# Two counting pairs in front of the gathered bodies, the preparing stage's waits moved into the next program, and the last stage of a graph kernel in one pass by quads

## The reference, cut to what matters

```python
# layer 0: message passing with a GRU cell
msg = (x[src] @ W_msg.T + b_msg) + edge_embed[clip(edge_type, 0, 8)]
messages = segment_sum(msg, dst, N)
x = layernorm(x + gru_cell(messages, x))
# layer 1: edges weighted by a gated score
proj = x @ fc_weight.T
el, er = proj[src], proj[dst]
e = sum(leaky_relu(el + er, 0.2) * a, -1)
w = sigmoid(e * sigmoid(sum(el * er, -1)))
neigh = segment_sum(x[src] * w, dst, N) / max(deg, 1)
x = layernorm(x + (1 + eps) * x + neigh)
```

## Time and profile before

| what | us |
|---|---|
| median of three runs | 3278.78 |
| lowest and highest | 3277.06 and 3279.28 |
| the profiled execution, its own time | 3269.84 |
| its span in the profile | 3268.0 |
| busy in the span: PE, DVE, ACT, POOL | 2154.1, 2508.1, 1592.7, 2135.2 |
| mean granted TensorE clock, as a share of full speed | 0.772 |

### The profile page before, as it was taken

One profiled execution on the slowest core, in us unless ns is written; L12 is line 12 of the kernel. 1 busy time (PEld: TensorE's weight loads), 2 busy tenths in 40 slices (PEclk: granted clock), 3 DMA queues, 4 the chain that ended last, 5 costly groups with the idle time before them and its releaser, 6 DMA issues. The chain is left out here.

```text
span 3268.0 us, 64802 instructions
## 1 busy us (share of the span) xinstructions
PE 2154.1 (66%) x13842; PEld 1733.9 (53%) x13842; DVE 2508.1 (77%) x12778; ACT 1592.7 (49%) x3458; POOL 2135.2 (65%) x2191
## 2 busy tenths in 40 slices
PE   1399999999989745555555555555655555555653
PEld 1277777777754445454444454454555545545552
DVE  6577777777735678888888888888888888888877
ACT  2265555555543345445445454445454544544541
POOL 2456766667720067777777777777777777777772
PEclk9999999999999766667667667767566666676665
DMA  7222222222220465655555565665565565566562
GB/s 142 79 57 65 73 65 70 71 67 70 68 71 1 146 182 158 168 163 158 168 163 158 165 166 158 162 166 161 159 170 161 158 167 164 157 169 164 155 169 65
DMA packets 357854, 424.88 MB, mean 130 GB/s; under 512 B 174156, under 2 KB 242134, under 8 KB 357733
## 3 DMA queue, kind: packets, MB, share of 16 engines
q0 software_dynamic: 103728, 266.13, 29.7%
q1 hardware_dynamic: 251793, 156.64, 18.3%
q10 hardware_dynamic: 2212, 0.60, 0.1%
HBM read 399.44 MB, written 23.70 MB: 129 GB/s over the span
## 5 line engine op out<-in xcount | busy, mean ns | idle before, releaser
L1407 POOL DMA_INDIRECT got<-rows,idx x1624 | 1546.5, 952 | 538.7 <-issue 509.8
L1573 PE MATMUL sum_ps<-whot,got 128*128 128x128 f32 x3264 | 690.1, 381 | 642.3 <-DVE whot L1419 573.2
L1573 PEld LDWEIGHTS sum_ps<-whot,got 128*128 128x128 f32 x3264 | 594.0, 273 | 730.5 <-DVE whot L1419 641.0
L735 POOL DMA_INDIRECT got<-x_rows,idx x532 | 540.5, 1016 | 255.9 <-issue 161.2
L1566 PE MATMUL er_ps<-win,hot_t 128*128 128x128 bf16 x4932 | 528.6, 285 | 260.7 <-ACT hot_t L1517 238.4
L886 ACT CAST work<-c_ps 128x318 bf16<-128x318 f32 x1092 | 454.9, 431 | 398.7 <-PE c_ps L962 391.1
L1475 DVE CUSTOM_DVE_ANT_0 pr_s<-got,er_ps 128x128 f32<-128x128 f32 x1624 | 370.0, 283 | 363.8 <-DMA got<-rows,idx 357.9
L1566 PEld LDWEIGHTS er_ps<-win,hot_t 128*128 128x128 bf16 x4932 | 468.9, 133 | 303.6 <-ACT hot_t L1517 268.2
L913 PE MATMUL span_ps<-x_parts,work 128*126 128x393 bf16 x2756 | 611.4, 332 | 0.0
L1419 DVE TENSOR_SCALAR whot<-iota_f,dl,w_s 128x128 f32<-128x128 f32 x1632 | 459.0, 358 | 0.3 <-ACT w_s L1522 0.3
L1547 ACT ACTIVATE r_s<-er_ps 128x512 f32<-128x512 f32 x406 | 242.3, 597 | 373.2 <-DVE er_ps L1487 371.2
(11 more groups left out here) (239 smaller groups left out, 1879.3 us busy)
## 6 DMA issues: line engine op xcount, KB each, us to landing
work<-dst_row SPq DMA_DIRECT2D x413, 256.0 KB, 4.0
got<-rows,idx POOLq DMA_INDIRECT x1624
win<-parts SPq DMA_DIRECT2D x118, 96.0 KB
got<-x_rows,idx POOLq DMA_INDIRECT x532
idx<-src_rows SPq DMA_DIRECT2D x413, 2.0 KB, 4.0
parts<-split SPq DMA_DIRECT2D x13, 384.0 KB, 2.9
x_rows<-x_parts SPq DMA_DIRECT2D x1, 4641.0 KB
rows<-nodes SPq DMA_DIRECT2D x13, 256.0 KB, 3.1
```

The lines of the kernel that those rows point to most:

```text
L735: pool.indirect_dma_start(got[:, c, i, 0:3 * D], None, x_rows, bass.IndirectOffsetOnAxis(ap=idx[:, c, i:i + 1], axis=0)).then_inc(gathered ...
L1407: pool.indirect_dma_start(got[:, c, i, :], None, rows, bass.IndirectOffsetOnAxis(ap=idx1[:, c, i:i + 1], axis=0)).then_inc(gathered[c], 16)
L1573: mm = pe.matmul(sum_ps[:, 0:P], got[:, c, i, D:2 * D], whot[:, c, i, :], start=(c == 0 and i == 0), stop=(c == NS - 1 and i == STEP - 1))
```

## The change

Five things are done.

1. SP stores `x_rows` in two halves, the first as soon as VectorE's first half is ready, and the three waits at the end of its program stand at the start of its next one. Three tables (`dst_t`, `type_h`, `src_i`) share the room of others, and `first_k` and its like live on into the next stage, since they are still being stored.
2. POOL clears `counts` first, waits for the earlier stores (which read `sums`' and `nodes`' room), and then clears `sums`.
3. LEAD = 2 pairs stand in front of the rounds and none behind them; the wait for the cleared tables is made by VectorE in the first pair that adds.
4. ScalarE multiplies `nodes` by `c_x` in front of its loop of the edge stage, 13 steps of a quad each.
5. The last stage is one pass: four PSUM buffers; product and sum in one step for each tile; the root of each quad by ScalarE, with the bound as its bias; reciprocal and offset by VectorE one quad later; and the normalising by ScalarE (scale and bias from the tables) two quads later, for the last quad by VectorE. POOL does nothing there.

The diff, cut to its core:

```diff
@@ preparing, SP @@
-                    sp.wait_ge(lo_cut, 2)
-                    sp.dma_start(x_rows[0:xf * LO, :].rearrange("(b p) f -> p b f", p=LO),
-                                 x_parts[0:LO, 0:xf, 0:3 * D]).then_inc(x_out, 16)
+                    for i, (b0, b1) in enumerate(half_b):
+                        bm = min(b1, xf)
+                        sp.wait_ge(lo_cut, i + 1)
+                        sp.dma_start(x_rows[b0 * LO:bm * LO, :].rearrange("(b p) f -> p b f", p=LO),
+                                     x_parts[0:LO, b0:bm, 0:3 * D]).then_inc(x_out, 16)
...
-                    sp.wait_ge(left_out, 16 * (2 + (br > 0)))
-                    sp.wait_ge(dst_out, 48)
-                    sp.wait_ge(tables_out, 48)
@@ counting, SP and POOL @@
+                    sp.wait_ge(left_out, 16 * (2 + (CT % ROWS > 0)))
+                    sp.wait_ge(dst_out, 48)
+                    sp.wait_ge(tables_out, 48)
...
                     pool.memset(nodes[:, ft:NTL, :], 0.0).then_inc(nodes_set, 1)
+                    pool.memset(counts[:, 0:NPAD], 0.0).then_inc(zeroed0, 1)
+                    pool.wait_ge(left_out, 16 * (2 + (CT % ROWS > 0)))
+                    pool.wait_ge(dst_out, 48)
                     pool.memset(sums[:, 0:NPAD], 0.0).then_inc(zeroed0, 1)
-                    pool.memset(counts[:, 0:NPAD], 0.0).then_inc(zeroed0, 1)
@@ counting, VectorE (ScalarE and PE alike) @@
                     make_pair(0, True)
-                    dve.wait_ge(zeroed0, 3)
+                    for k in range(1, LEAD):
+                        make_pair(k, False)
                     with dve.Fori(0, ROUNDS) as r:
                         for p in range(ROUND):
-                            make_pair(ROUND * r + p + 1, False, p, r)
-                    with dve.Fori(ROUNDS * ROUND + 1, PAIRS) as k:
-                        make_pair(k, False)
+                            make_pair(ROUND * r + p + LEAD, False, p, r)
@@ edges, ScalarE @@
+                    for q in range(NQ):
+                        t = slice(q * QUAD, (q + 1) * QUAD)
+                        act.activation(nodes[:, t, :], nodes[:, t, :], ACT.Copy, scale=c_x[:]).then_inc(scaled, 1)
                     with every_body(act) as k:
@@ last stage, ScalarE, VectorE and SP as they are now @@
+                    def root(q):
+                        act.wait_ge(agreed, QUAD * (q + 1))
+                        act.activation(rstd[:, q * QUAD:(q + 1) * QUAD], moments[:, q * QUAD:(q + 1) * QUAD, 1],
+                                       ACT.Sqrt, bias=low_bound[:]).then_inc(rooted, 1)
...
+                    def normalise(q):
+                        act.wait_ge(shifted, q + 1)
+                        for t in range(q * QUAD, (q + 1) * QUAD):
+                            act.activation(nodes[:, t, :], nodes[:, t, :], ACT.Identity, scale=rstd[:, t:t + 1],
+                                           bias=offset_s[:, t:t + 1]).then_inc(finished_act, 1)
...
+                    for q in range(NQ):
+                        root(q)
+                        if q >= 2:
+                            normalise(q - 2)
+                    normalise(LAST - 1)
...
+                    def scale_of(q):
...
+                        dve.wait_ge(rooted, q + 1)
+                        dve.reciprocal(rstd[:, t], rstd[:, t]).then_inc(inverse, 1)
+                        dve.wait_ge(inverse, q + 1)
+                        dve.scalar_tensor_tensor(out=offset_s[:, t], in0=moments[:, t, 0], scalar=-1.0,
+                                                 in1=rstd[:, t], op0=ALU.mult, op1=ALU.mult).then_inc(shifted, 1)
...
+                        for i in range(QUAD):
+                            t = q * QUAD + i
+                            dve.scalar_tensor_tensor(out=nodes[:, t, :], in0=m_ps[:, q % 4, i, :],
+                                                     scalar=rdeg[:, t:t + 1], in1=nodes[:, t, :],
+                                                     op0=ALU.mult, op1=ALU.add).then_inc(mixed, 1)
...
+                        if q >= 1:
+                            scale_of(q - 1)
...
+                    scale_of(LAST)
+                    dve.wait_ge(shifted, NQ)
+                    for t in range(LAST * QUAD, NTL):
+                        dve.tensor_scalar(nodes[:, t, :], nodes[:, t, :], rstd[:, t:t + 1], offset_s[:, t:t + 1],
+                                          ALU.mult, ALU.add).then_inc(finished, 1)
...
+                    for at in range(0, ft, 4):
+                        m = min(4, ft - at)
+                        wait_for(at + m)
+                        sp.dma_start(out[at * NODES:(at + m) * NODES, :].rearrange("(t p) f -> p t f", p=NODES),
+                                     nodes[:, at:at + m, :]).then_inc(stored, 16)
```

More of the change, by code:

```diff
@@ L48 @@
 PER_ROUND = 3
+LEAD = 2
 LN_EPS = 1e-5
@@ L897, in _ @@
                     copy_pair(0, True)
+                    for k in range(1, LEAD):
+                        copy_pair(k, False)
                     with act.Fori(0, ROUNDS) as r:
                         for p in range(ROUND):
-                            copy_pair(ROUND * r + p + 1, False, p, r)
-                    with act.Fori(ROUNDS * ROUND + 1, PAIRS) as k:
-                        copy_pair(k, False)
+                            copy_pair(ROUND * r + p + LEAD, False, p, r)
                     copy_sums(CGN - 2, 0)
@@ L980, in _ @@
                     count_pair(0, True)
+                    for k in range(1, LEAD):
+                        count_pair(k, False)
                     pe.wait_ge(zeroed0, 3)
@@ L1599, in graph_layers @@
         with ExitStack() as ph:
-            mean_s = sb("mean_s", [NODES, QUAD, D], F32, ph)
-            m_ps = psum("m_ps", [NODES, 2, QUAD, D], F32, ph)
+            m_ps = psum("m_ps", [NODES, 4, QUAD, D], F32, ph)
+            low_bound = sb("low_bound", [NODES, 1], F32, ph)
+            offset_s = sb("offset_s", [NODES, NTL], F32, ph)
+            bound_set = sem("bound_set")
             m_turned = sem("m_turned")
-            steps = sem("steps")
-            spread = sem("spread1")
+            mixed = sem("mixed")
+            stated = sem("stated")
+            agreed = sem("agreed")
+            rooted = sem("rooted")
+            inverse = sem("inverse")
+            shifted = sem("shifted")
             finished = sem("finished")
+            finished_act = sem("finished_act")
             stored = sem("stored")
-            finished_pool = sem("finished_pool")
-            S = 2 + 2 * QUAD
-            HERE = NTL * 3 // 4 // QUAD * QUAD + QUAD if NQ > 4 else NTL
-            def normalise(eng, tiles, done):
-                for t in tiles:
-                    eng.tensor_scalar(nodes[:, t, :], nodes[:, t, :], moments[:, t, 0:1], rstd[:, t:t + 1],
-                                      ALU.subtract, ALU.mult).then_inc(done, 1)
+            LAST = NQ - 1
             with nc.Block() as block:
@@ L1652, in _ @@
-                    dve.wait_ge(steps, S * NQ + 1)
-                    dve.tensor_scalar(rstd[:], moments[:, :, 1], LN_EPS, None, ALU.add).then_inc(spread, 1)
-                    dve.wait_ge(spread, 2)
-                    dve.reciprocal(rstd[:], rstd[:]).then_inc(spread, 1)
-                    dve.wait_ge(spread, 3)
-                    dve.sem_inc(spread, 1)
-                    normalise(dve, range(0, HERE), finished)
-                @block.gpsimd
-                def _(pool):
-                    pool.wait_ge(spread, 4)
-                    normalise(pool, range(HERE, NTL), finished_pool)
+                            dve.wait_ge(mixed, q * QUAD + i + 1)
@@ L1667, in _, with wait_for @@
                     n = 0
-                    starts = sorted(range(0, ft, 4), key=lambda t: t - (HERE if t >= HERE else 0))
-                    for at in starts:
+                    def wait_for(tiles):
+                        sp.wait_ge(finished_act, min(tiles, LAST * QUAD))
+                        if tiles > LAST * QUAD:
+                            sp.wait_ge(finished, tiles - LAST * QUAD)
+                    for at in range(0, ft, 4):
                         m = min(4, ft - at)
-                        if at >= HERE:
-                            sp.wait_ge(finished_pool, at - HERE + m)
-                        else:
-                            sp.wait_ge(finished, at + m)
+                        wait_for(at + m)
                         sp.dma_start(out[at * NODES:(at + m) * NODES, :].rearrange("(t p) f -> p t f", p=NODES),
```

67 lines of the change are left out of this document (30 added, 37 removed).

## The result

The changed kernel takes 3261.86 us, median of 7 executions, beside 3277.06 for the kernel before, timed together with it: ratio 0.9946 (0.9934 to 0.9957), 17.7 us less (14.1 to 21.6). The ratio is an estimate from all executions; the two medians alone differ by 15.2 us. Timed again later, the pair came to 0.9966 (0.9952 to 0.9979), 11.1 us less (6.9 to 15.7), 3259.01 beside 3270.95. The second time the kernel before ran 6.1 us faster than the first, the changed one 2.9.

A forecast was written before the change was run, and what follows sets the result against it. PE bounds the rounds, POOL's gathers the edge stage, VectorE the last stage, SP's store queue the seam. Terms 0 + 3.2 - 13.0 = -9.8 us from 3278.78 give 3269.0; range 3265 to 3273, eight in ten 3261 to 3277.

The forecast's parts named there:

- Seam, -6.9: After preparing: splitting the x_parts store ends it 3.7 us earlier, moving three waits saves 3.2; together 6.9 us.
- the transfer is the same bytes from the same partitions, so it ends 3.7 us earlier: Seam's store: the first half is ready 3.7 us sooner, so the whole transfer ends that much earlier.
- Rival E: Seam: halves slowed or a second large store costs SP, PE starts up to 3.7 us later; 3273; chance 0.10.
- Two pairs in front, 0: End of counting: the left-over body's gathers, no longer under the lone pair, give back the seam's 6.9 us: 0.
- rival D: Left-over body's bursts: the clock drops and stays low into the update stage; with 40 us, 3289; chance 0.05.
- B: Rival at counting's end: left-over gathers start earlier, seam's 6.9 us stay; -16.7, 3262; sign: products end by 945; chance 0.14.
- Edge stage, +3.2: Start of edge stage: 13 ScalarE scalings, 8.0 us, delay VectorE; POOL pauses once, near 1190: +3.2 (1.5 to 4.9).
- Last stage, -13.0: Last stage in one pass: quads of 2.64 us, then ScalarE's root and eight steps; -13.0 us (-15 to -11).
- 0.47 for four aggregations: Last stage: part of VectorE's old quad of 2.76 us, kept at 0.47 us in the new quad of 2.64.
- Rival C: Last stage: narrow steps cost full length, quad 3.1 us, 6 us more than forecast; -4, 3275; chance 0.15.

The follow-up runs named there:

- the run of the pairs alone: The kernel before with two pairs in front of the rounds and none behind, nothing else: ratio 1.0036 (1.0023 to 1.0050), 11.8 us slower.
- the first eight runs: Follow-up runs up to the combined kernel, in which every kernel, that before included, took about 4.28 ms; ratios between 0.9939 and 0.9995.
- one of the texts above: Text of the timing run of the kernel before with VectorE's loop of rounds 112 instructions further on: ratio 1.0006 (0.9996 to 1.0017).

## Why the prediction was right and wrong

The sign was right, and so were the waits and paths that the sum names; its sizes were off, that of the last stage by most. By its own steps:

- **Seam, -6.9.** Right where halves drain as slowly as one store (SP held 39.4 and 39.9 us in two profiles: counting 7.5 and 6.9 us earlier after the first dst_left store), too small by up to 5 us in the others. The step that failed is "the transfer is the same bytes from the same partitions, so it ends 3.7 us earlier": in seven of eleven profiles the halves held SP for under 36 us, not 39. Rival E, a slower transfer, is refuted.
- **Two pairs in front, 0.** This was 6.9 won less 6.9 given back. The wait for the left-over gathers came as described; its size was off. Last gather 30.4 us behind body 17's sums instead of 29.3, the last seven products 2.2 us after its end instead of 1.3, these products 2.5 us long instead of 1.64 at the low clock, and 2.3 us more at low clock in the update stage (granted 0.51 from 941 to 950), which I had priced only in rival D: 11.8 us given back in the run of the pairs alone, not 6.9. Of four bursts two ran together. The rest of the seam's gain stays, and the last products ended at 940.56, before the 945 that the forecast had named as B's sign. So B's time was met, but not by B's mechanism: in all eleven profiles of kernels of some 3.25 ms the last gather ends 29.1 to 30.8 us behind body 17's sums.
- **Edge stage, +3.2.** The working holds: 8.05 us of scalings for 8.0, a wait of 10.18 for 11, 3.2 us of pauses. But POOL stood still twice, 2.0 and 1.2 us, where the forecast had one pause and called a second a sign against it. Over all profiles the gathers took 4.4 us more.
- **Last stage, -13.0.** The largest error: 18.4, from 72.9 and 54.5 us behind the last gather. The quad was priced at 2.64 and took 2.36. The step that failed is "0.47 for four aggregations", taken over at their old price: up to the next quad's first step they now take 0.29 us. The reciprocal and the narrow product in front of them are not the reason, since the first quad, which has neither, takes 0.28 too (3211.63 to 3211.91). The 0.47 held a wait: before, the next quad's product waited by `steps` for all aggregations and started 0.11 us after their end (3214.73, then 3214.84). Now it waits for PE alone and starts 0.08 us before their end (3214.35, then 3214.27). This is read from the waits and times of the two kernels; no run puts that one wait back. A product took 0.25 instead of 0.275. 13 quads times 0.28 are 3.6 us. The last root and ScalarE's eight steps took 3.4 us (3240.23 to 3243.64) instead of 3.7. From ScalarE's last step to the end are 4.2 us instead of the 5.2 of the forecast (3249.8 to 3255.0), and the stage began 0.4 us sooner behind the last gather. Rival C went the wrong way.
- **Rival D, the clock,** had its first step: 0.57 over 26 us. It came back at 950, as the forecast argued, and cost 2.3 us in the update stage, 2.1 by the mean of all profiles.

Measured term by term the change is 12.7 us for the last stage with the scalings, 11.8 more for the seam (24.5 - 12.7), 11.8 back for the pairs: 12.7, between its two timings. Each of these terms is uncertain by some 4 to 6 us. The profiled execution had a short store and short rounds and was the shortest of its seven; whether the others, and so the recorded 17.7, owe anything to the same is not shown. Of the 8 us between forecast and record the last stage gives 5.4, the edge stage takes 1.2, the seam gives up to 5, the pairs take 5 more than thought; what is left, some 4 us, is less than the two timings of the same kernel differ.

## What to carry to other kernels

Before a transfer is split in time or started earlier, read its share of the DMA engines: 0.43 said that two lines (a cut at 112 partitions) were worth at least as much as the whole change. Work that is moved from behind a loop to its front uncovers what it lay on; price that by the last thing it waits for, with landing and low clock. And a difference of 5 us between two profiled executions is no term until a second profile of the same kernel has it: here the rounds of one kind differed by 6 us.

## What the runs showed of the hardware that was not expected

At a jump back VectorE stood idle for 1.7 to 4.8 us (591 instructions a round), by where its loop begins, and PE for 1.8 to 3.3 us; the trace puts it down as "issue" on VectorE, and on PE as a wait for the engine whose semaphore came last. In the first eight runs, on two chips, the kernel before took 4.28 ms instead of 3.27, and for long stretches each of PE's matmuls came 2.8 us after the last, idle time that ended with nothing the profile shows (timeline of the first run's PE; columns as above):
```profile
1716.63 0.27 PE L1568 MATMUL er_ps<-win,hot_t 128*128 128x128 bf16 x1 [2.53 <-issue]
1719.44 0.27 PE L1568 MATMUL er_ps<-win,hot_t 128*128 128x128 bf16 x1 [2.54 <-issue]
```
That PE received its instructions slowly, as one of the texts above has it, is a reading of these rows; the cause was not looked for. A store at a DMA share of 0.43 moved 120 GB/s, one at 0.96 moved 278.
